# Adding a mixture of experts' rows into the output itself instead of into a copy

## What is computed

```python
scores = sigmoid(xf @ gate_w.T)                 # xf: 2048 tokens x 512, layer-normed
idx = top 4 of 16 experts, out of the 2 best groups of 4, after a bias
cw[token, idx] = w / sum(w)                     # weights of the chosen experts, else 0
h = silu(einsum('td,edh->teh', xf, w1)) * einsum('td,edh->teh', xf, w3)
y = einsum('teh,ehd,te->td', h, w2, cw)         # each token: 4 experts of width 352
z = silu(xf @ sw1) * (xf @ sw3) @ sw2           # a shared expert of width 704
x = x + tanh(g_ffn[1]) * (y + z)
```

## Time and profile before

| | us |
|---|---|
| runs of the kernel before | 1370.13, 1370.34, 1373.58 (median 1370.34) |
| the profiled execution | 1371.29, span 1369.6, mean granted clock of PE 0.954 |
| block of routing and shared expert | 583.6 to 845.9 |
| block of the expert tiles | 845.9 to 1369.5 |
| share of the span with PE busy | 90% |

### The profile page before, as it was taken

The page is one execution under the profiler, slowest core; times in us unless marked ns, Lnnn a source line. Parts: engine busy times, 40 slices in busy tenths (PEclk is TensorE's granted clock), DMA queues, the critical chain, the costliest instruction groups (busy, mean ns, idle before and its releaser), DMA issues. The chain is left out here.

```text
span 1369.6 us, 25480 instructions
## 1 busy us (share of the span) xinstructions
PE 1230.6 (90%) x7821; PEld 1034.4 (76%) x7822; DVE 719.2 (53%) x1443; ACT 553.2 (40%) x1430; POOL 424.0 (31%) x504
## 2 busy tenths in 40 slices
PE   6998999999997399969998998699999989999992
PEld 6876777777776177746776876699999878999992
DVE  5666655656645589953677643442334443424340
ACT  4543444444444188833121111543344443434341
POOL 1101211211211556540005721235444433444442
PEclk9999999999998699979999999899999999999997
DMA  9000000000000111143000204555446755545456
GB/s 326 25 16 19 17 1 18 17 1 17 1 2 1 33 45 38 38 141 118 0 1 0 94 31 137 159 129 100 77 80 141 195 142 116 132 86 135 86 140 169
DMA packets 53880, 103.62 MB, mean 76 GB/s; under 512 B 5126, under 2 KB 20998, under 8 KB 53750
## 3 DMA queue, kind: packets, MB, share of 16 engines
q1 hardware_dynamic: 38182, 65.78, 14.7%
q0 software_dynamic: 15632, 36.97, 14.3%
HBM read 75.99 MB, written 30.93 MB: 78 GB/s over the span
## 5 line engine op out<-in xcount | busy, mean ns | idle before, releaser
L1738 PE MATMUL t_H<-m_W,t_xT 128*128 128x352 f32 x1632 | 286.4, 332 | 16.7 <-DVE m_W L1816 13.9
L1738 PEld LDWEIGHTS t_H<-m_W,t_xT 128*128 128x128 f32 x1632 | 268.0, 193 | 18.7 <-DVE m_W L1816 14.8
L1705 POOL DMA_INDIRECT acc_d<-t_ys,t_sid x68 | 109.2, 1606 | 279.0 <-ACT t_ys L1767 191.5
L1783 ACT ACTIVATE t_sl<-t_H 128x352 f32<-128x352 f32 x68 | 31.5, 463 | 175.4 <-PE t_H L1738 173.7
L597 ACT ACTIVATE pr<-pr 128x128 f32<-128x128 f32 x256 | 76.0, 298 | 55.2 <-DVE pr L758 53.9
L62 PE MATMUL t_Y<-m_W,t_hT 128*128 128x512 f32 (+1 forms) x207 | 88.2, 426 | 9.4 <-DVE t_hT L1861 6.4
L1837 DVE TENSOR_TENSOR t_h<-t_H,t_sl 128x352 f32<-128x352 f32 x68 | 35.5, 523 | 106.5 <-ACT t_sl L1783 106.5
L1767 ACT ACTIVATE t_ys<-t_Y,t_wcol 128x512 f32<-128x512 f32 x69 | 47.3, 685 | 94.8 <-PE t_Y L64 94.8
L1859 DVE TENSOR_TENSOR t_hT<-t_TH,t_hT 128x256 fp32r<-128x256 f32 x68 | 28.7, 422 | 107.1 <-ACT t_hT L1804 105.9
L64 PE MATMUL t_Y<-m_W,t_hT 128*128 128x512 f32 (+1 forms) x207 | 82.3, 397 | 0.0
L63 PE MATMUL t_Y<-m_W,t_hT 128*128 128x512 f32 (+1 forms) x207 | 82.0, 396 | 0.0
(11 more groups left out here) (415 smaller groups left out, 3229.6 us busy)
## 6 DMA issues: line engine op xcount, KB each, us to landing
m_r<-in_L_ffn_w_dram SPq DMA_DIRECT2D x26, 704.0 KB, 5.1
m_r<-in_L_ffn_w_dram SPq DMA_DIRECT2D x13, 512.0 KB, 3.9
aCX<-in_ctx_dram SPq DMA_DIRECT2D x20, 256.0 KB, 2.6
rows_d<-before_w SPq DMA_DIRECT2D x17, 256.0 KB, 2.0
CT<-in_ctx_dram SPq DMA_DIRECT2D x8, 512.0 KB, 3.8
X<-in_x_dram SPq DMA_DIRECT2D x4, 1024.0 KB, 13.0
acc_d<-X SPq DMA_DIRECT2D x4, 1024.0 KB, 4.2
m_r<-in_L_ffn_sw_dram SPq DMA_DIRECT2D x4, 704.0 KB, 5.4
```

Of the source, the lines that this page charges most:

```text
L1705: pool.indirect_dma_start(out=m["acc_d"][:, :], out_offset=bass.IndirectOffsetOnAxis(ap=sid[:, b:b + 1], axis=0), in_=ys[:, b, :], in_offs ...
L1738: x_ = pe.matmul(bk[b % 2][:, 0:I], xT[:, b % 2, jx, k, :], W13[:, jw, k, j, :], start=k == 0 and jx == jw, stop=k == KC - 1 and jx == 1)
```

## The change

`acc_d` goes away; what was stored and added there is stored and added in the output (`out_rows`), which has 2048 rows and no pad rows. So an empty slot needs a real row to add its zeros to, and one which no other slot of the same accumulating DMA names. For slot p of expert e's last tile a token of the first block of 128 tokens is taken: one that expert e was not given (or, if e has 128 tokens or more, simply token p; tiles past the last expert's take token p as well). Steps:

- `spots()` on DVE at q = 8: five operations of 128x16. `tile_experts` on DVE at q = 10: three more (17x80, and two of 128x17x17 in bf16).
- POOL makes for each of the 16 experts a one-hot 128x128 in bf16 that says which token sits at which slot (`spot_at`, two buffers, taken in turn), after its tables and before its wait for `table_out`.
- PE sums 16 + 1 small products in `spare_tokens()`, called first thing in `outer_last`; one more, `spare_rows()`, between the two pairs of `outer_last`. DVE copies the first result out between, and makes `target`, the rows to add to, in `targets()` (four operations of 128x80).
- SP stores three groups of X; the fourth is stored by POOL at the start of the next block, in place of the pad rows' zeroing. The final copy is gone.

```diff
@@ routing_and_shared_expert: tiles
+        spot, far_spot, spot_row = c["mean"], c["rstd"], c["onesF"]
+        small = sb_[:, :, :].rearrange("p t e -> p (t e)").bitcast(BF16)
+        spread = small[:, 0:(E + 1) * (E + 1)].rearrange("p (e f) -> p e f", e=E + 1)
+        tile_of = small[0:E + 1, 304:304 + NT]
+        spot_at = [selB[:, 8 * n:8 * n + 8, :].rearrange("p t e -> p (t e)") for n in range(2)]
+        spare_of, spare_t, spare_j = triB[0:E + 1, :], CP[0:E + 1, 0:P], CP[:, P:P + NT]
@@ SP
-                for g in range(NG):
+                for g in range(NG - 1):
                     sp.wait_ge(y_out, GB * (NU - NG + g + 1))
-                    sp.dma_start(m["acc_d"][g * GT:(g + 1) * GT, :].rearrange("(b p) d -> p b d", p=P),
+                    sp.dma_start(m["out_rows"][g * GT:(g + 1) * GT, :].rearrange("(b p) d -> p b d", p=P),
                                  X[:, g * GB:(g + 1) * GB, :]).then_inc(stored, 16)
@@ POOL
                 step(pool.tensor_copy(iP, iPi))
+                step(pool.tensor_copy(spot_row[:, :], iPi))
...
                 step(pool.tensor_copy(m["rowid"][:, NT:NT + UT], m["pads"]))
+                pool.wait_ge(spare_ok, 2)
+                for e in range(E):
+                    wait(pool, spot_used, e - 1)
+                    pool.tensor_scalar(spot_at[e % 2], spot_row[:, :], spot[:, e:e + 1], None, ALU.is_equal).then_inc(spot_set, 1)
                 pool.wait_ge(table_ok, 1)
@@ PE
+                def spare_tokens():
+                    pe.wait_ge(spare_ok, 2)
+                    for e in range(E + 1):
+                        if e < E:
+                            pe.wait_ge(spot_set, e + 1)
+                        i = pe.matmul(spare_t, spread[:, e, :], spot_at[e % 2] if e < E else c["identB"][:, :],
+                                      start=e == 0, stop=e == E)
+                        if e < E:
+                            i.then_inc(spot_used, 1)
+                    i.then_inc(spare_ps, 1)
+                def spare_rows():
+                    pe.wait_ge(spare_ok, 3)
+                    pe.matmul(spare_j, spare_of, tile_of, start=True, stop=True).then_inc(spare_ps, 1)
                 def outer_last(u):
                     b = u // NG
+                    spare_tokens()
                     for pair in range(GB // 2):
+                        if pair == 1:
+                            spare_rows()
@@ DVE
+                def spots():
+                    count = run[:, 0, NB - 1, :]
+                    dve.wait_ge(iotas, 6)
+                    step(dve.scalar_tensor_tensor(out=spot[:, :], in0=count, scalar=tok[:, 0:1], in1=PT[:, 0:E],
+                                                  op0=ALU.add, op1=ALU.subtract))
+                    step(dve.scalar_tensor_tensor(out=spot[:, :], in0=sel[:, 0, :], scalar=-float(T_ALL), in1=spot[:, :],
+                                                  op0=ALU.mult, op1=ALU.add))
+                    step(dve.tensor_scalar(far_spot[:, :], spot[:, :], -1.0, tok[:, 0:1], ALU.mult, ALU.add))
+                    step(dve.scalar_tensor_tensor(out=far_spot[:, :], in0=count, scalar=P - 0.5, in1=far_spot[:, :],
+                                                  op0=ALU.is_gt, op1=ALU.mult))
+                    dve.tensor_tensor(spot[:, :], spot[:, :], far_spot[:, :], ALU.add).then_inc(spare_ok, 1)
+                def targets():
+                    dve.wait_ge(spare_ps, 2)
...
                 def tile_experts():
...
+                    step(dve.tensor_scalar(tile_of, ej[0:E + 1, 0:NT], tok[0:E + 1, 0:1], None, ALU.is_equal))
+                    both = [P, E + 1, E + 1]
+                    step(dve.tensor_tensor(spread, iJ[:, 0:E + 1].unsqueeze(1).to_broadcast(both),
+                                           iJ[:, 0:E + 1].unsqueeze(2).to_broadcast(both), ALU.is_equal))
+                    dve.tensor_scalar(spread, spread, tok[:, 0:1], None, ALU.mult).then_inc(spare_ok, 1)
...
+                            if q == 8:
+                                spots()
...
+                    if u == NU - 1:
+                        dve.wait_ge(spare_ps, 1)
+                        dve.tensor_copy(spare_of, spare_t).then_inc(spare_ok, 1)
                     for t in range(GB):
+                        if u == NU - 1 and t == 2:
+                            targets()
@@ expert_tiles: SP
                 sp.wait_ge(sc_done, trips * (16 * UT) + 16)
                 sp.sem_inc(own_sp, 1)
-                sp.dma_start(out.rearrange("b p d -> (b p) d"), m["acc_d"][0:T_ALL, :]).then_inc(out_done, 16)
-                sp.wait_ge(out_done, 16)
@@ expert_tiles: POOL
-                pool.memset(zpad[:, :], 0.0).then_inc(padded, 1)
-                pool.wait_ge(padded, 1)
-                pool.dma_start(m["acc_d"][T_ALL:T_ALL + PADS, :], zpad[:, :]).then_inc(sc_done, 16)
+                last = slice((NG - 1) * GT, NG * GT)
+                pool.dma_start(m["out_rows"][last, :].rearrange("(b p) d -> p b d", p=P), c["X"][:, (NG - 1) * GB:NG * GB, :])\
+                    .then_inc(sc_done, 16)
...
-                pool.wait_ge(m["stored"], 16 * NG)
+                pool.wait_ge(m["stored"], 16 * (NG - 1))
...
-                            pool.tensor_copy(sid[:, b:b + 1], rowid[:, bass.ds(n, 1)]).then_inc(zeroed, 1)
+                            pool.tensor_copy(sid[:, b:b + 1], m["target"][:, bass.ds(n, 1)]).then_inc(zeroed, 1)
```

More of the change, by code:

```diff
@@ L968, in experts @@
     rows_d = nc.dram_tensor("rows_d", [T_ALL + PADS, D], F32, kind="Internal").ap()
-    acc_d = nc.dram_tensor("acc_d", [T_ALL + PADS, D], F32, kind="Internal").ap()
     with ExitStack() as st:
@@ L973, in experts @@
         m = dict(meta=sb("m_meta", [1, 3, NT + 3], I32),
-                 pos=sb("m_pos", [P, NB, 8]), vals=sb("m_vals", [P, NB, TOPK, 3]), rows_d=rows_d, acc_d=acc_d,
+                 pos=sb("m_pos", [P, NB, 8]), vals=sb("m_vals", [P, NB, TOPK, 3]), rows_d=rows_d, out_rows=out.rearrange("b p d -> (b p) d"),
                  stored=st.enter_context(nc.semaphore("stored")),
@@ L981, in experts @@
         places = m["pos"].rearrange("p t n -> p (t n)")
+        m["target"] = m["vals"].rearrange("p t k a -> p (t k a)")[:, 0:NT].bitcast(U32)
         m["gid"], m["pads"] = places[:, 0:UT].bitcast(U32), places[:, UT:2 * UT].bitcast(I32)
         routing_and_shared_expert(nc, c, m, gate_w, ebias, w1, w2, w3, sw1, sw2, sw3)
-        expert_tiles(nc, c, m, w1, w2, w3, out)
+        expert_tiles(nc, c, m, w1, w2, w3)
 def load_expert(sp, m, w1, w3, e, done):
@@ L1088, in routing_and_shared_expert @@
         x13_in, x2_in, x13_hi = sem("ex13_in"), sem("ex2_in"), sem("ex13_hi")
+        spare_ok, spot_set, spot_used, spare_ps = (sem(f"e_{n}") for n in ("spare_ok", "spot_set", "spot_used", "spare_ps"))
         tab_a_set, tab_b_set, tab_used = (sem(f"e_{n}") for n in ("tab_a_set", "tab_b_set", "tab_used"))
@@ L1504, in table_out @@
                     step(dve.tensor_tensor(m["wgt"][:, 0:NT], L[:, 2 * NT:3 * NT], m["wgt"][:, 0:NT], ALU.add))
+                def targets():
+                    dve.wait_ge(spare_ps, 2)
+                    spare, away = iJ[:, 0:NT], c["bst"].rearrange("p a b -> p (a b)")[:, 0:NT]
+                    step(dve.tensor_scalar(spare, spare_j, -float(T_ALL), None, ALU.add))
+                    step(dve.scalar_tensor_tensor(out=away, in0=L[:, 0:NT], scalar=tok[:, 0:1], in1=spare,
+                                                  op0=ALU.add, op1=ALU.subtract))
+                    step(dve.scalar_tensor_tensor(out=away, in0=L[:, 0:NT], scalar=0.0, in1=away, op0=ALU.is_lt, op1=ALU.mult))
+                    dve.scalar_tensor_tensor(out=m["target"], in0=away, scalar=float(T_ALL), in1=spare,
+                                             op0=ALU.add, op1=ALU.add)
                 def tile_experts():
@@ L1602, in _, with expert_tiles @@
                                                  in1=X[:, tt, :], op0=ALU.mult, op1=ALU.add).then_inc(y_out, 1)
-def expert_tiles(nc, c, m, w1, w2, w3, out):
+def expert_tiles(nc, c, m, w1, w2, w3):
     identF = c["identF"]
@@ L1628, in expert_tiles @@
         TX, TH = bank("t_TX", 1)[0], bank("t_TH", 1)[0]
-        zpad = sb("t_zpad", [PADS, D])
-        wcol_set, zeroed, padded = sem("wcol_set"), sem("t_zeroed"), sem("t_padded")
+        wcol_set, zeroed = sem("wcol_set"), sem("t_zeroed")
         r13_in, r2_in, w13_hi, w13_lo, w2_hi, w2_lo = (sem(f"t_{n}") for n in ("r13_in", "r2_in", "w13_hi", "w13_lo", "w2_hi", "w2_lo"))
@@ L1636, in expert_tiles @@
         g_in = m["g_in"]
-        sc_done, out_done = sem("t_sc_done"), sem("t_out_done")
+        sc_done = sem("t_sc_done")
         own_pool, own_act, own_dve, own_sp = c["passed_pool"], c["passed_act"], c["passed_dve"], c["passed_sp"]
@@ L1704, in _ @@
                             pool.sem_inc(own_pool, 1)
-                            pool.indirect_dma_start(out=m["acc_d"][:, :],
+                            pool.indirect_dma_start(out=m["out_rows"][:, :],
```

## The result

The changed kernel takes 1376.51 us (median of 20 runs, 1371.06 to 1380.47). The kernel before, run beside it, takes 1370.61 (20 runs, 1365.13 to 1376.84). The ratio is 1.0037, with a 95% interval from 1.0023 to 1.0052: 5.1 us slower, by 3.2 to 7.1. The forecast was a sum of +5.4. The profiled execution of the changed kernel has a span of 1376.8 us, against 1369.6 before: 7.2 more.

The account below looks back on a forecast made before the run. PE, busy for 90% of the span, bounds the kernel, with the final copy holding the end. Terms 2.1 + 10.6 + 2.4 - 0.5 + 0.8 - 10.0 = +5.4 gave 1375.7 us against the median; range 1368.5 to 1383.0.

Parts of the forecast that it names:

- The end, -10.0: Program end: without the final copy, POOL's last drain is late next, so the end moves from 1369.6 to 1359.6.
- DVE at q = 8 and q = 10, +2.1: Routing block: the added DVE steps lengthen PE's waits by 1.05 us at each of two places, both in full.
- POOL's copy, 0: POOL's extra 128x128 copy, before its tables: about 0.60 us, hidden by its wait for PE; at worst 0.6.
- The one-hots, +10.6: Before the last unit: PE waits for 14 POOL compares at 0.60 (8.4), plus 1.5 and 0.7; bounds 4.7 to 14.7.
- My 1.5 for DVE beside POOL: Part of the stall before the last unit: 1.5 us added because DVE's work slows the first five compares.
- The rule of the Trainium skill: One-input POOL operations run at roughly line rate; would bring about the quick-compare rival, stall 4.7, total 1369.8, chance 0.13.
- The clock, +2.4: Last unit: PE, nearly idle before it, starts at clock 0.50 for 4.4 to 6.3 us; +2.7, less 0.3.
- the clock holds: Rival at the last unit: the 17 small matmuls count as work enough, sum +2.7, 1373.0; chance 0.12.
- The block's end, -0.5: End of routing block: the meeting no longer waits for SP to issue the last store after DVE's last addition.
- POOL's store, +0.8: Start of next block: POOL's later 1 MB store delays the next expert's weights; bounds -0.7 and +4.2.
- The tiles, 0: The 68 accumulating DMAs keep their shape with another target; no row gives a reason for a different landing time.
- The gathers and the small DVE steps, hidden: Around the last unit: later first gathers have some 6 us to spare; 1.1 us of DVE steps fit its 3.23 wait.

Follow-up runs that it names:

- b_nocopy: The kernel before without its final copy from accumulator to output, so the output is never written: 1361.51 us, ratio to before 0.9935.
- b_dve: The kernel before plus only the change's eight DVE operations at q = 8 and q = 10, results unread: 1373.63 us, ratio to before 1.0034.
- a_filler: The changed kernel with two idle 512-column matmuls before each product from the third to the sixteenth: 1376.95 us, ratio to before 1.0036.
- a_spstore: The changed kernel with the last 1 MB store back on SP and a 1 KB DMA by POOL instead: 1374.58 us, ratio to before 1.0018.
- a_early: The changed kernel with `spots` moved to q = 7 and two of the three q = 10 steps to q = 18: 1372.6 us, ratio to before 1.0018.
- best: The changed kernel with products in pairs between earlier tiles, DVE steps moved, last store on SP: 1363.29 us, ratio to before 0.9943.

## Why the prediction was right, point by point

The forecast's case came about (+5.4 by the sum, +5.1 by the timed runs), but some of its terms were off, and the total hides that.

- **The end, -10.0:** -9.8. Reading which instruction is late next, and taking its duration from beside the copy, was enough; b_nocopy shows that the copy had no part in that duration.
- **DVE at q = 8 and q = 10, +2.1:** the waits are what I worked out (1.04 and 1.11 longer), and all of it reaches PE. **This is the term that failed.** I priced the wait and not what it does to the clock. It is +2.8 at the last unit's place in the changed kernel's profile and +4.5 in b_dve. The step "both in full +2.1" took the two waits as time alone, though further down, for the last unit, I read from the earlier trace rows that a wait of 3.3 brings the clock down. I had no row between 1.42 and 3.3, and should have put the upper bound of this term at two low stretches. That the total came out so near is luck in part: behind the second wait the clock held in the changed kernel's profile and fell in the four others with such a wait, which made PE some 1.7 to 1.9 later. (The three steps at q = 10 also add up to 1.08 in the working, not 1.05; measured are 1.11.)
- **POOL's copy, 0:** hidden, as seen in POOL's wait of 26.59 us for PE behind it. The copy took 1.49 us, where I had priced 0.60.
- **The one-hots, +10.6:** 9.8. The compare is 594 ns with a bf16 output, the same as with fp32r. My 1.5 for DVE beside POOL was too much: one of 14 took 1.6 us, so it was 14 in 9.10. The rule of the Trainium skill (GPSIMD Engine Reference, section 4.1, Engine selection) that one-input operations go at about line rate is not borne out for this operation: 594 ns for 128 columns, against 288 of the other one-input operation of bf16.
- **The clock, +2.4:** +2.5. a_filler shows the cause: with work in the gap it stays at 1.00, and the unit takes 9.2. The lower level lasted 5.9 us of the unit, within the 4.4 to 6.3 that I took from the earlier trace rows. But this length is not fixed by the kernel: behind the same gap of 9.8 it was 5.9 again in a_spstore (the unit took 11.8) and only 2.5 in a_early (10.3). The rival "the clock holds" fell; its price was off by 0.3, since it takes away 2.7 where the term was 2.4, so it stood for 1373.3 and not 1373.0.
- **The block's end, -0.5:** the meeting follows DVE's last addition by 0.2 instead of 0.7.
- **POOL's store, +0.8:** 1.2, right in kind; the load beside it took 8.22 instead of 6.32.
- **The tiles, 0:** -0.9, within what one profile varies.
- **The gathers and the small DVE steps, hidden.** Both are as the prediction had them, and the rows below show it.

POOL's timeline has the two gathers at

```profile
850.65 1.23 POOL L1001 DMA_INDIRECT m_first<-rows_d,m_pos  x1 [0.86 <-POOL m_pos L1195]
852.18 0.96 POOL L1001 DMA_INDIRECT m_first<-rows_d,m_pos  x1 [0.30 <-issue]
```

and PE's first tile begins at 862.69, after a wait for the block's meeting and not for them. `targets` and the last additions in DVE's timeline, against the 3.23 of the earlier trace rows:

```profile
857.59 0.23 DVE L1557 TENSOR_SCALAR r_iJ<-eC 128x80 f32<-128x80 f32 x1
...
860.90 1.46 DVE L1671 SCALAR_TENSOR_TENSOR X<-eY,tg,X 128x512 f32<-128x512 f32 x2 [2.20 <-PE eY L64]
```

DVE still idles 2.20 us before them. By phases from the first addition, the changed kernel's profile has 14.6 + 1.2 - 0.9 - 9.8 = +5.1. The sum's own terms for the same phases were 14.6 (2.1 + 10.6 + 2.4 - 0.5), 0.8, 0 and -10.0: DVE's 0.7 too little and the one-hots' 0.8 too much cancel.

## What to carry to other kernels

Work given to an idle engine is not free when the engine that bounds the kernel must take each product at one point of its own list: 14 compares of 0.6 us, all asked for at one place, cost 12 us of PE, and the same compares asked for two at a time between tiles cost 3. When a step is put in front of a wait of the matrix engine, price the wait and then ask what clock the engine restarts with; in b_dve the second part was nearly as large as the first (2.15 and 2.35). And before counting on a removed tail, find the instruction that is late next, on every engine's list.

## What the runs showed of the hardware

- **Waits and the clock.** PE's waits at the two DVE places and the granted clock behind them, over nine kernels: after 1.20 to 1.75 us it never fell (before, b_nocopy, a_early, best); after 2.24 or 2.25 at q = 8 it fell in all five that had such a wait; after 2.53 to 2.74 in the unit after, in four of five (in the changed kernel's own profile not). Why that one held is open. I did not try lengths between 1.75 and 2.24. The length of the wait alone does not decide it. At unit 0 all nine kernels have the same wait of 1.57 us, behind twelve small matmuls; the clock fell behind it in three (a_filler, b_nocopy, best) and held in six. These are PE's row and the stretch of `best`; the kernel before has 1.00 at this place:

```profile
638.11 0.41 PE L62 MATMUL eL<-XT,egwT 128*16 128x512 f32 x1 [1.57 <-DVE XT L1643]
...
638.00:640.00 2.00, 1.89 (x6) 0.75 (x7) 1.30 (x3) 0.63 (x1) 0.00 (x0) 0.64 0.14 35
```

- **POOL's drain.** At the end of the last block it took 4.07 us in the five kernels in which SP issues the last store of X and 4.23 in the four in which POOL does, and 3.66 at the end of the routing block, where the changed kernel's record of it, 4.90, spans the issue of both gathers (the second to 853.1) and ends 2.6 after it:

```profile
L1117 POOLq DRAIN  x1: 4901/4901/4901, 850.9 to 850.9; - x1
```

The copy is not its cause. Whether the gathers and accumulating DMAs that POOL itself issues are its cause was not tried.
- **Small matmuls among large ones.** Two bf16 matmuls of 128 columns between 512-column fp32 ones cost 0.39 us, though each alone is 0.06 of column time at 0.233 per 512 columns: 0.12 for both. What the other 0.27 is, the trace does not split; a change of type and of weights stands on either side of the pair.
